# State-space scan on one core: in every second state TensorE multiplies the turned input by a diagonal of B

## What is computed

```
delta = softplus(dt_raw @ dt_proj_w.T + dt_proj_b)         # (b, t, 256)
dA  = exp(einsum('bti,is->btis', delta, A))
dBu = einsum('bti,bts->btis', delta * u, B_ssm)            # 16 states s
h   = dA_t * h + dBu_t                                     # over t
y_t = einsum('bis,bs->bi', h, C_t)
y   = (y + u * D_param) * silu(z);  return y @ out_proj_w.T + residual
```

## Time and profile before

| | |
|---|---|
| median of 3 runs | 1367.31 us (1366.61 to 1368.74) |
| the profiled execution | 1359.86 us, span 1358.1 us |
| busy in the span: TensorE, VectorE, ScalarE, GpSimd | 80%, 70%, 66%, 38% |
| mean granted TensorE clock | 0.923 |

### The profile page before, as it was taken

How to read it: one execution, slowest core, us unless ns; L and a number is a source line. 1 busy time by engine, 2 the same in 40 slices (tenths; PEclk the granted TensorE clock), 3 DMA queues, 4 the chain that set the end, 5 groups by cost and what they waited for, 6 DMA issues and landing times. The chain is left out here.

```text
span 1358.1 us, 26011 instructions
## 1 busy us (share of the span) xinstructions
PE 1087.7 (80%) x7230; PEld 732.7 (54%) x7230; DVE 957.2 (70%) x2037; ACT 898.7 (66%) x1865; POOL 513.2 (38%) x318
## 2 busy tenths in 40 slices
PE   1776488878788787863895899999999999992697
PEld 1333366666666675651894345454454445541696
DVE  5899577778788788854664467685776768673465
ACT  1787698989889798941673466665766566660564
POOL 0467377677767767861443000101101010111244
PEclk9888699899899899977998799999999999995899
DMA  3000132223254235321332100000000000000321
GB/s 83 2 3 2 32 87 86 74 84 93 78 173 133 91 116 156 90 67 51 95 94 63 47 1 1 17 1 17 13 3 16 1 16 0 16 17 33 97 88 49
DMA packets 50616, 74.26 MB, mean 55 GB/s; under 512 B 7351, under 2 KB 28604, under 8 KB 50528
## 3 DMA queue, kind: packets, MB, share of 16 engines
q1 hardware_dynamic: 41504, 51.09, 13.2%
q0 software_dynamic: 5568, 12.66, 2.6%
q10 hardware_dynamic: 3456, 9.46, 2.3%
HBM read 57.86 MB, written 16.24 MB: 55 GB/s over the span
## 5 line engine op out<-in xcount | busy, mean ns | idle before, releaser
L951 DVE TENSOR_TENSOR_SCAN h<-d_a,p_dbu 128x1024 f32<-128x1024 f32 x128 | 291.0, 2282 | 79.3 <-ACT d_a L738 55.4
L685 POOL TENSOR_TENSOR h<-h,c_rep 128x1024 f32<-128x1024 f32 x128 | 301.5, 2366 | 113.9 <-DMA c_rep<-c_rows 71.1
L1833 ACT ACTIVATE at_probs<-at_scores,at_min 128x512 f32<-128x512 f32 x256 | 183.7, 722 | 136.0 <-DVE at_min L1943 87.0
L1195 POOL DMA_INDIRECT expert_rows<-r_row,r_dest x64 | 62.9, 982 | 503.7 <-DVEq L1121 488.2
L1943 DVE CUSTOM_DVE_ANT_0 at_scores<-at_p_scores,arena 128x512 f32<-128x512 f32 x256 | 174.4, 684 | 89.8 <-PE at_p_scores L1709 50.2
L828 PE MATMUL p_dbu<-ident,b_du_T 128*128 128x128 f32 x1024 | 189.6, 306 | 55.4 <-ACT b_du_T L731 52.9
L731 ACT ACTIVATE b_du_T<-arena,b_T 128x256 f32<-128x256 f32 (+1 forms) x512 | 216.9, 496 | 0.3 <-ACT arena L712 0.2
L828 PEld LDWEIGHTS p_dbu<-ident,b_du_T 128*128 128x128 f32 x1024 | 117.2, 150 | 119.9 <-issue 66.8
L738 ACT ACTIVATE d_a<-arena,a_exp 128x511 f32<-128x511 f32 (+1 forms) x256 | 169.3, 710 | 0.7 <-DVE h L951 0.6
L1716 PE MATMUL at_p_probs_T<-ident,at_probs 128*128 128x128 f32 x1024 | 158.9, 283 | 5.3 <-ACT at_probs L1833 4.6
L1716 PEld LDWEIGHTS at_p_probs_T<-ident,at_probs 128*128 128x128 f32 x1024 | 112.7, 142 | 91.2 <-issue 68.0
(11 more groups left out here) (211 smaller groups left out, 1484.1 us busy)
## 6 DMA issues: line engine op xcount, KB each, us to landing
c_rep<-c_rows SPq DMA_DIRECT2D x128, 256.0 KB, 3.3
f_row<-expert_rows SPq DMA_DIRECT2D x78, 129.0 KB
arena<-in_w_all ACTq DMA_DIRECT2D x8, 578.0 KB, 4.0
arena<-bias_by_distance ACTq DMA_DIRECT2D x8, 448.0 KB, 3.8
x_tok<-in_x SPq DMA_DIRECT2D x4, 512.0 KB, 5.4
x_tok<-x_between SPq DMA_DIRECT2D x8, 256.0 KB, 2.8
expert_rows<-f_pad SPq DMA_DIRECT2D x10, 129.0 KB, 3.1
expert_rows<-f_pad ACTq DMA_DIRECT2D x8, 129.0 KB, 3.1
```

The costliest lines, as they stand in the source:

```text
L685: nc.gpsimd.tensor_tensor(h[:, s % HS, :, :], h[:, s % HS, :, :], cc, ALU.mult).then_inc(prod_done, 1)
L951: nc.vector.tensor_tensor_scan(h[:, s % HS, :, :].rearrange("p c t -> p (c t)"), da[:, s % 2, :, :].rearrange("p c t -> p (c t)"), p_dbu[: ...
L1833: nc.scalar.activation(pr[:, s % 2, :], sc[:, s % 2, :], ACT.Exp, scale=-1.0, bias=mn[:, s % 2:s % 2 + 1]).then_inc(probs_ready, 1)
```

## The change

In states with odd s, `scale` no longer multiplies the turned input (128 x 256). It multiplies the identity (128 x 128) by the column of B and so makes a 128 x 128 diagonal, in the same buffer. `spread` then multiplies du_T (as the stationary operand) by this diagonal in plain float32 matmuls, where it transposed before. Even states stay as they are. Semaphores, their counts and the order stay.

```
@@ scale(b, s)
                 for j in range(TPB):
-                    nc.scalar.activation(b_du[:, s % SR, j, :], du_T(b, j), ACT.Copy,
+                    src, n = (k.ident[:], P) if s % 2 else (du_T(b, j), DI)
+                    nc.scalar.activation(b_du[:, s % SR, j, 0:n], src, ACT.Copy,
                                          scale=bT[:, one(b), j, s:s + 1].squeeze(1)).then_inc(scaled, 1)
@@ spread(b, s)
                     for ch in range(NC):
-                        mm = nc.tensor.transpose(p_dbu[:, s % 2, ch, j * P:(j + 1) * P],
-                                                 b_du[:, s % SR, j, ch * P:(ch + 1) * P], k.ident[:])
+                        dst = p_dbu[:, s % 2, ch, j * P:(j + 1) * P]
+                        if s % 2:
+                            mm = nc.tensor.matmul(dst, du_T(b, j)[:, ch * P:(ch + 1) * P], b_du[:, s % SR, j, 0:P],
+                                                  start=True, stop=True)
+                        else:
+                            mm = nc.tensor.transpose(dst, b_du[:, s % SR, j, ch * P:(ch + 1) * P], k.ident[:])
                 mm.then_inc(dbu_ready, 1)
```

## The result

The changed kernel takes 1371.97 us (median of 12 runs, 1368.17 to 1378.24); the kernel before, run again beside it, 1366.55 us (12 runs, 1362.5 to 1370.01). The ratio is 1.0041, with a 95% interval of 1.0024 to 1.0057: 5.6 us slower, 3.3 to 7.8. That is inside the range of 1361 to 1377, and beyond the 0.2% that I had held likeliest: rival 3's side. So the two spans, 1369.8 and 1358.1 us, differ by more than the kernels do, and pieces have to be compared, not totals.

A forecast was written before the change was run, and what follows sets the result against it. No engine bounds the scan throughout: ScalarE paces piece A, TensorE piece B, router round trips piece C. Six batches +6.6, batch 0 -0.9, batch 7 -0.3, clock -3.4 make +2.0 us: 1369.3 us, range 1361 to 1377.

The forecast's parts named there:

- rival 3: Slower: TensorE becomes the bound, piece A gains under 0.4 us, clock returns under 2; 1380, or about 1374; chance 0.37.
- Prices of one odd state: ScalarE saves 107 ns per `scale` instruction, four times per odd state; an odd `spread` costs TensorE 0.95 us more.
- rival 4: Slower: a plain matmul costs the page's factor of four, an odd `spread` 3.5 us; 54 us more, 1421; chance 0.01.
- Piece B: Gate (s = 2) to scan of s = 8: TensorE paces, two odd spreads uncovered, +1.9 us a batch.
- Batch 7: Last batch: turns no next `du`, end paced by GpSimd, so only a share of piece A's gain, -0.3 us.
- Piece A: Calm part, s = 13 to 3 of the next batch: ScalarE paces; gain 0 to 1.28 us, taken as 0.8 a batch.
- Batch 0: First batch, no gate before it: slow start +1.3 us, then six odd scalings -2.1; together given as -0.9.
- Clock: TensorE's clock, gate to gate: filling idle time may make drops fewer, worth 0 to -6.8 us; half taken, -3.4.
- piece C: s = 8 to 12: router round trips over VectorE, ScalarE, TensorE; odd spreads fall in TensorE's idle time, effect 0.
- Rival 1: Faster: the clock stays up, all drops in piece C vanish, piece A gives its full 1.28; about 1363; chance 0.19.
- Idle time before `spread` of s = 10: TensorE's wait in piece C: the odd `spread` of s = 9 fills 0.95 us, leaving 1.3 us where 2.31 was.
- GpSimd: Rate limit of its products, 3.0 us a state: no gate-to-gate stretch can fall much below 52 to 53 us.

The follow-up runs named there:

- the two kernels with and without s = 5 and 7: Kernel before with only s = 5 and 7 changed: ratio 1.0100, 13.7 us slower; changed kernel with those two left as before: 0.9984, 2.2 us faster.
- short products: GpSimd's products cut to 8 of 512 elements per chunk, in four kernels; before 1337.13 us, changed 1340.18, changed without s = 5 and 7 1329.72.
- ScalarE's saving alone: Kernel before, but odd states scale 128 columns, transposed twice, second chunk's input left out: ratio 0.9977; with short products 1324.99 us.
- split ones: Each GpSimd product as two 128 x 512 instructions, nothing left out; against the kernel before: before split 0.9955, changed split 0.9974.

## Why the prediction was right or wrong

The range held the time; the likeliest case, no measurable change, was wrong, and rival 3 (slower, 0.37) came true in sign, at 5.6 us where it said 6 to 13. Its mechanism came true by half: the clock returned nothing, but TensorE did not become the bound of the calm part, which gained 0.64 us. Step by step:

- *Prices of one odd state*: right. ScalarE saved 108 ns an instruction, and `scale` begins 2.82 and 2.39 us after the last by turns, as foretold. A plain spread costs 0.91 us more. The factor of four of the Trainium skill ("TensorE: Matmul & The Clock Gate", Terms), on which rival 4 stood, is refuted once more: 1.79 against 0.88 us, a factor of 2.0.
- *Piece B, +1.9 us*: the right mechanism, shown by the two kernels with and without s = 5 and 7. The size is 1.54 us with short products, 1.68 with whole ones, both in batch 3. In the latter the first spread gave its whole 0.91 and the second 0.77, because TensorE had waited 0.16 us for VectorE's sum (L966) before the turn at L809, and after the change it waited no more; and my 0.95 was a little high.
- *Batch 7*: I gave it -0.3 and no loss behind the gate. With short products its piece B grew by 1.0 us (16.53 to 17.55) and gate to gate by 0.8. No next `du` is turned there, but the spread of s = 5 still stands before L857. That was a slip.
- *Piece A, -0.8 us*: -0.64 with short products, from 20.1 to 19.5. Right mechanism and nearly the size. ScalarE's saving alone gives 1.4 in most batches (20.1 to 18.7), so TensorE's odd spreads, that of s = 3 among them, take half of it back; that the one at s = 3 is the cause was not resolved.
- *Batch 0, -0.9*: -1.7 from first scan to gate with short products (55.6 to 53.9 us). The loss at its start, where I put 1.3, did not come: scan of s = 0 to scan of s = 8 was 24.33 us before and 24.37 after. My two terms, +1.3 and -2.1, make -0.8, not -0.9.
- *Clock, -3.4*: the step that failed. I read the spread of lengths in the earlier trace rows as the price of the lower clock. The clock did rise, to 0.97, and nothing came back, because it had fallen where TensorE waited anyway: piece C takes 14.73 us at 0.93 and at 1.00. Its extra length came from router operations that wait for GpSimd. That the low clock follows from this fits the order in batch 3 (VectorE's L1073 is late at 347.39, TensorE idles for 2.31 us before 349.87, and its transposes are slow from 351.25 on), but it is not the only way, since the clock also fell in kernels without such waits. Rival 1 rested on the same misreading. Where the clock was seen to cost time is piece B, 1.6 us, and piece A with ScalarE's saving alone, 0.7. In piece B both kernels ran at full clock, so the change had nothing to win back there.
- *Idle time before `spread` of s = 10*: 2.19 us after, where I read 2.31 and expected 1.3. The odd `spread` of s = 9, drawn out by its waits for ScalarE's parts, took 1.86 us where the even one had taken 1.38 (start to start of `sum_up`): it filled 0.48 us and not 0.95, and the chain behind it came 0.25 us later.
- *GpSimd*: I took it only as a rate limit, and L1109's 1.55 us as a number that "does not get shorter". It is a 0.19 us operation in the way of a product. This was the largest thing missed: most of the 28 us that short products take off, about 5 of them being the rate limit at the end of batch 7, which I had right.

Without the clock term the sum would have been +5.4. Part of that agreement is luck: with short products the profiles give six stretches +5.0, batch 0 -1.7, batch 7 +0.8, together +4.1, and the medians +3.0. With whole products it is +5.6 (3.3 to 7.8), with split ones +2.6. Whether whole products make the changed kernel's waits worse than those of before, or the difference of 2.6 us is measurement, stays open: the interval's lower end is 3.3, and the waits of the two profiles, 44.5 and 33.1 us, come from one execution each, that of before a fast one. Shown is that GpSimd's whole products take most of a gain: 12.1 us became 3.1, and 7.4 became 2.2. How much of this is VectorE's waits, and how much the lower clock in piece B that comes only with whole products, is not separated.

## What to carry to other kernels

Moving work from the busiest engine to another pays only in the states where the busy one paces; where the other's queue stands unbroken behind a gate, each added microsecond is lost, so make such a change by state and not by parity. When an operation's duration varies tenfold (0.17 and 2.05 us here), look at what another engine runs at that moment before looking at clocks. A low clock beside a long stretch need not be its cause: compare the same piece at both clocks, and each piece by itself. Here the same fall cost nothing where TensorE waited for others and 1.6 us where its queue stood unbroken.

## What was unexpected in the hardware

- Some of VectorE's small operations wait for the end of a running GpSimd instruction: 0.17 to 2.3 us for 128 x 4 elements, 1.09 to 3.3 us for four of 128 x 128. Cutting GpSimd's instructions short took 28 us (2%) off, about 5 of them at the end of batch 7, where its products pace.
- Halving them did not halve the waits, as a train of VectorE's operations can meet several (3.0 to 4.6 us for L1078's four in five batches of seven), and one operation can wait through several: 2.77 and 4.39 us where a half takes 1.28.
- The lower clock cost 1.6 us in a piece where TensorE paced (17.98 against 16.38 us) and nothing in one where it did not (14.73 us at both).
- In three further sessions, on different chips, the kernel before took 1366.3, 1366.7 and 1378.5 us in the median. In the second of them its nine runs spread over 6.7 us; with short products five runs spread over 4.1, and five of the changed kernel with short products over 1.1.
